# First cross-attention maxima put directly behind the self attention, paired cross units, and four setup products moved to the prologue

## The chip, the core and the metric

The kernel runs on one core of a Trainium2 chip. A core has five engines that run side by side and meet at semaphores: PE (TensorE, matrix products), DVE (VectorE), ACT (ScalarE), POOL (GpSimd) and SP, which here only issues transfers. The metric is device time in microseconds (us) of the whole kernel. Products are written to PSUM, 8 banks of 128 partitions x 512 f32, and read from there by ACT and DVE.

## The reference

Two layers on x of shape (2, 1024, 256) with a context of shape (2, 77, 256):

```python
# layer 0
x = attention(ln32(x), ln32(x), Wq1, Wkv1, Wo1, bo1) + x      # 16 heads of 16, self: 1024 x 1024
x = attention(ln32(x), context, Wq2, Wkv2, Wo2, bo2) + x      # 16 heads of 16, cross: 1024 x 77
x = geglu_ff(ln32(x), Wff1, bff1, Wff2, bff2) + x             # 256 -> 2 x 1024 -> 256
# layer 1
Q = x @ Wq.T + bq; K = ctx @ Wk.T + bk; V = ctx @ Wv.T + bv   # one head of 256
x = rms_norm(softmax(Q K^T / 16) V @ Wfc.T + bfc + x, norm_w)
```

Both softmaxes of layer 0 subtract the row maximum, which the kernel computes beforehand in a first pass of score products.

## The kernel before

The 2048 tokens are 4 blocks of 512 (16 tiles of 128). The 2 x 16 heads are 8 groups of 4 heads, groups 0 to 3 for the first batch, 4 to 7 for the second. The program is written out by hand, one instruction list for each engine, and each list runs in its order; the lists meet at counted semaphores. The stages, with their place in the profiled execution:

- Prologue (0 to 80 us): loads, first layer norm, projections of q, k and v, which go to scratch memory through SP's queue and come back by head. The first 22 tiles of self scores (`first_scores`) lie between them.
- Self attention (80 to 440 us): for each group 16 steps of four transposed score tiles (L915), exponentials (ACT, L1308) and weighing (L927); beside them the score tiles and maxima (L746, DVE L1562) of the next group.
- Cross attention (440 to 563 us). For a group G: four `scores_2` (L1022) with a maximum each (`reduce_2`, DVE L1780); `split_max` (L1568, L1570) turns the result into two halves; `turn_max_2` (L1058) transposes it; `max_copy_2` (ACT L1359) copies it to mT; `load_max_2` (SP L532, two transfers) puts it below the queries in the stack, and only then may `scores_t2` (L1033) of that group start. Its product goes through the exponential (`exp_2`, ACT L1366), `weigh_2` (L1041), a copy (L1372), a transpose (`turn_out_2`, L1052) and `attended_2` (DVE L1718, L1724).
- Feed-forward (563 to 717 us), with each product taken as three of reduced-precision parts, so weights and inputs are split into high and low halves beforehand (`w1_high` on ACT L1342, `w1_low` on DVE L1766, wff2 on POOL L619 and L621). Then layer 1 to 752 us.

Between the attentions and the layer after them stands the chain: a generator `chain(n, b)` for attention n and batch b, from which the engines take pieces at places given by tables. A piece is the transposes of a block (L699; before the products they turn the attention's output, after them the normalised tokens), one product of a tile with Wo (L888, on DVE followed by an addition and the statistics of the norm), or, for n = 0, one projection of the cross queries (`project`, L713; ACT L1223 and DVE L1551 write it, SP L444 stores it, and SP L460 loads it by head, `load_q2`). The DVE's norm steps for a block are short, and are fed one at a time into its list by `tick()`; `finish_norm()` runs what is left of them. The cross stage has units, 8 to a group; PIECES_1 and PIECES_2 say how many pieces follow each unit, AHEAD and FIRST_S2 how many stand ahead of the first. The nine setup products of layer 1 (`final_setup`, L828) are fed in at SETUP_UNITS. Scores of the cross units alternate between two PSUM banks, 4 and 5. A group's q is loaded into one of four slots, so groups 4 to 7 wait until the slot is free.

SP's queue is strictly in order too, so a load waits behind whatever the queue waits for; `parts_stored` holds it until stores have landed.

## Time and profile before

| | us |
|---|---|
| median of 3 runs | 752.19 (751.94 to 753.55) |
| the profiled execution, its own time | 753.79 |
| its span, first to last instruction | 751.8 |
| PE busy | 666.3 (89%) |
| DVE busy | 542.8 (72%) |
| ACT busy | 496.7 (66%) |
| POOL busy | 81.0 (11%) |

The span is 2.0 us below the execution's own time, which is 1.6 us above the median. Busy shares are means over the whole kernel: a stage is read from the table by stretch and the timeline.

### The profile page before, as it was taken

What the parts mean: (1) busy time and instruction counts of PE and PEld (TensorE: products, weight loads), DVE (VectorE), ACT (ScalarE), POOL (GpSimd) and SP (SyncE); (2) the same over time, 40 slices, a digit from 0 to 9 for tenths busy, and PEclk for the clock granted to TensorE, in tenths of its full rate; (3) what the DMA queues carried; (4) which work ended last, traced back from release to release, by engine and by line L of the source; (5) the groups of instructions that cost most, each with busy time, mean ns of one, the idle gap of its engine ahead of it and who ended that gap; (6) DMA issues with size and microseconds to landing.
All of it is one profiled execution on the core that took longest, in us unless ns stands there. A gap on an engine that the chain in (4) does not pass through costs nothing.

```text
span 751.8 us, 11175 instructions
## 1 busy us (share of the span) xinstructions
PE 666.3 (89%) x4072; PEld 319.0 (42%) x4072; DVE 542.8 (72%) x937; ACT 496.7 (66%) x893; POOL 81.0 (11%) x124
## 2 busy tenths in 40 slices
PE   4989799999999999999999873989979999999981
PEld 2644122222222222222224341445537888888870
DVE  6778989999999999999973548465654954343367
ACT  3543299999999999999998730666664333233374
POOL 2080800000000000000000203200020110000004
PEclk9999699999999999999999996899968999999995
DMA  9567440202020100001000021121000000000003
GB/s 295 186 194 230 103 183 1 72 1 71 1 71 2 47 26 1 29 2 29 2 2 1 29 76 38 54 59 34 3 1 1 0 1 1 1 1 1 1 0 112
DMA packets 35114, 36.87 MB, mean 49 GB/s; under 512 B 6133, under 2 KB 28277, under 8 KB 34805
## 3 DMA queue, kind: packets, MB, share of 16 engines
q1 hardware_dynamic: 33904, 35.87, 15.3%
q0 software_dynamic: 1024, 0.24, 0.3%
q8 instruction: 32, 0.52, 0.3%
q14 instruction: 22, 0.17, 0.1%
q10 hardware_dynamic: 132, 0.07, 0.0%
HBM read 23.09 MB, written 12.74 MB: 48 GB/s over the span
## 4 chain that ended last, share of the span: by engine, by line
PE 66%; DVE 15%; ACT 11%; issue 5%; POOL 1%; DMA 0%; ACTq 0%; SPq 0%; DVEq 0%; POOLq 0%
PE ps L927 15%; PE ps L915 10%; DVE mm L1562 7%; ACT probs L1308 6%; PE ps L713 6%; PE ps L1112 4%; PE ps L1113 4%; PE ps L1114 4%; PE ps L746 3%; PE ps L888 3%; PE ps L699 2%; PE ps L1041 2%; PE ps L1128 2%; PE ps L1127 2%; PE ps L1129 2%
## 5 line engine op out<-in xcount | busy, mean ns | idle before, releaser
L1308 ACT ACTIVATE probs<-ps,unfit 128x512 f32<-128x512 f32 x512 | 311.7, 691 | 27.9 <-PE ps L915 23.4
L1562 DVE TENSOR_REDUCE mm<-ps 128x2 f32<-128x1024 f32 x256 | 299.5, 1219 | 14.8 <-PE ps L746 10.8
L915 PE MATMUL ps<-stack 50*128 50x512 f16 x512 | 147.2, 389 | 7.0 <-ACT probs L1308 1.0
L927 PE MATMUL ps<-probs,v 128*32 128x512 f32 x1024 | 138.0, 611 | 2.7 <-ACT outT L1313 2.7
L746 PE MATMUL ps<-stack 48*128 48x512 f16 x512 | 109.1, 392 | 12.7 <-DVE mm L1562 6.6
L915 PEld LDWEIGHTS ps<-stack 50*128 50x128 f16 x512 | 36.9, 93 | 173.0 <-ACT probs L1308 164.1
L1421 ACT ACTIVATE early<-ps,cols 128x512 f32<-128x512 f32 x32 | 22.1, 690 | 90.8 <-PE ps L1114 90.8
L1831 DVE SCALAR_TENSOR_TENSOR hid<-ps,cols,early 128x512 f32<-128x512 f32 x32 | 24.0, 750 | 70.7 <-PE ps L1114 70.5
L1366 ACT ACTIVATE probs<-ps,unfit 96x512 f32<-96x512 f32 x64 | 42.2, 681 | 25.5 <-PE ps L1033 25.2
L1112 PE MATMUL ps<-x_hi,wff_hi 128*128 128x512 f32 x128 | 52.6, 411 | 0.0
L1113 PE MATMUL ps<-x_lo,wff_hi 128*128 128x512 f32 x128 | 51.2, 400 | 0.0
L1114 PE MATMUL ps<-x_hi,wff_lo 128*128 128x512 f32 x128 | 50.9, 398 | 0.0
L746 PEld LDWEIGHTS ps<-stack 48*128 48x128 f16 x512 | 26.2, 94 | 54.3 <-DVE mm L1562 30.5
L612 POOL TENSOR_TENSOR x<-x,rows 128x1024 f32<-128x1024 f32 x12 | 28.2, 2357 | 186.1 <-DVE tok L1540 186.0
L927 PEld LDWEIGHTS ps<-probs,v 128*32 128x32 f32 x1024 | 20.7, 108 | 41.2 <-issue 30.7
L1127 PE MATMUL ps<-wff_hi,hid_hi 128*128 128x256 f32 x128 | 36.4, 285 | 0.0
L1128 PE MATMUL ps<-wff_lo,hid_hi 128*128 128x256 f32 x128 | 36.1, 282 | 0.0
L1657 DVE TENSOR_TENSOR x<-ps,x 128x256 f32<-128x256 f32 x48 | 19.0, 418 | 23.5 <-PE ps L888 21.1
L888 PE MATMUL ps<-wo,wkv 128*128 128x256 f32 x128 | 33.6, 394 | 2.6 <-ACT wkv L1207 1.6
L1129 PE MATMUL ps<-wff_hi,hid_lo 128*128 128x256 f32 x128 | 35.8, 279 | 0.0
L1780 DVE TENSOR_REDUCE mm<-ps 128x8 f32<-128x616 f32 x32 | 25.5, 797 | 12.1 <-PE ps L1022 11.5
L646 POOL TENSOR_SCALAR mu<-mm 128x16 f32<-128x16 f32 x13 | 3.3, 254 | 287.1 <-DVE mm L1578 287.1
(168 smaller groups left out, 875.4 us busy)
## 6 DMA issues: line engine op xcount, KB each, us to landing
v_groups<-early SPq DMA_DIRECT2D x8, 512.0 KB, 3.1
stack<-q_parts SPq DMA_DIRECT2D x64, 64.0 KB, 2.1
v<-v_groups SPq DMA_DIRECT2D x8, 512.0 KB, 4.1
x<-in_x SPq DMA_DIRECT2D x4, 512.0 KB, 8.0
q_parts<-probs SPq DMA_DIRECT2D x8, 256.0 KB, 4.0
k_parts<-probs SPq DMA_DIRECT2D x8, 256.0 KB, 2.2
stack<-k_parts SPq DMA_DIRECT2D x16, 128.0 KB, 2.6
stack<-q_parts SPq DMA_DIRECT2D x64, 32.0 KB, 1.9
```

What stands on the lines that cost most here:

```text
L746: mm_ = eng.matmul(ps[:, 2 * s_slot(G, j, i) + tile, :], qs[rows_i, slot, half, q, P * t:P * t + P], stack[rows_i, SLOTS + slot, q, BLK * ...
L888: mm_ = eng.matmul(ps[:, out_bank(k), 0:D], attT[i // TPB][:, c, P * t:P * t + P], w[:, c, :], start=(c == 0), stop=(c == NC - 1))
L915: eng.matmul(ps[:, st_bank(n), :], stack[rows_of(tile, KROWS), SLOTS + slot, q, P * kc:P * kc + P], qs[rows_of(tile, KROWS), slot, half, q ...
L927: mm_ = eng.matmul(ps[32 * h:32 * h + 32, PV, :], v1[:, G % 2, kc, 32 * h:32 * h + 32], probs[:, k % 2, h, :], start=(kc == 0), stop=(kc = ...
L1112: eng.matmul(ps[:, bank, :], wh, xh[:, c, :], start=(c == 0), stop=False)
L1113: eng.matmul(ps[:, bank, :], wh, xl[:, c, :], start=False, stop=False)
L1114: mm_ = eng.matmul(ps[:, bank, :], wl, xh[:, c, :], start=False, stop=(c == NC - 1))
L1127: eng.matmul(out, hh, w2h, start=(f == 0), stop=False)
L1128: eng.matmul(out, hh, w2l, start=False, stop=False)
L1129: mm_ = eng.matmul(out, hl, w2h, start=False, stop=(f == FC - 1))
L1308: eng.activation(probs[:, k % 2, HEADS[h], :], ps[:, st_bank(n), :], ACT.Exp, scale=unfit[:, 0:1]).then_inc(exp_done, 1)
L1562: eng.tensor_reduce(dst, ps[:, 2 * slot:2 * slot + 2, :], AX.X, ALU.max).then_inc(s_red, 1)
```

## The change

Five things are edited.

1. Behind the self attention the first `scores_2` come after one chain piece (before: after six), and five pieces stand ahead of the first unit (before: ten). Queries of groups 0 and 1 are loaded in two halves, each as soon as its block is stored.
2. A cross unit is now a pair of heads: two products into banks 4 and 5 and one exponential over both (96 partitions x 1024). There are four units to a group, and the products of a unit wait until the exponential of the unit before has read both banks. `scores_2` run six units ahead; the weighing and turning of a group are placed anew, and the maximum of group G + 1 is turned in unit 2 of group G (before: unit 2 of 8).
3. The four k and v products of `final_setup` are moved to the prologue, with their copies on ACT instead of DVE; the other five to the units of group 7.
4. The split of wff1 moves from ACT and DVE to POOL, behind POOL's split of wff2. POOL adds the bias in pieces of two tiles instead of four.
5. The last group's second half and the last piece of the chain for batch 0 are moved behind the first feed-forward product. The feed-forward's own pieces start two products later.

```diff
-        CHAIN_1, CHAIN_2 = 17, 12
-        TAIL = (1, 1, 1, 1, 1, 2, 1, 2, 1, 2, 2, 2)
-        AHEAD, FIRST_S2 = 6, (0, 1, 0, 1, 0, 1, 0, 1) + (0,) * 8
...
-        UNITS = 8
...
-        PIECES_1 = ((1, 0, 1, 0, 1, 0, 1, 0), (1, 0, 1, 0, 1, 0, 0, 0))
-        PIECES_2 = ((0, 0, 0, 0, 0, 0, 0, 1), (1, 0, 1, 0, 1, 0, 1, 0), (1, 0, 1, 0, 1, 0, 1, 0), (1, 0, 1, 0, 1, 0, 0, 0))
-        SETUP_UNITS = ((2, 1), (2, 3), (2, 5), (3, 0), (3, 2), (3, 4), (3, 6), (4, 1), (4, 3))
-        FF_PIECES = (1, 2, 2, 2, 2, 1, 1, 1)
+        CHAIN_1, CHAIN_2 = 16, 12
+        TAIL = (1, 1, 1, 2, 2, 1, 2, 1, 1, 2, 1, 1)
+        UNITS = 4
+        S2_LEAD = 6
+        AHEAD = 5
+        PIECES = ((1, 1, 1, 1), (1, 1, 1, 2), (1, 1, 0, 0), (0, 0, 0, 0),
+                  (0, 0, 1, 1), (1, 1, 1, 2), (1, 1, 1, 1), (0, 0, 0, 0))
+        SETUPS = {(7, 0): 1, (7, 1): 2, (7, 2): 1, (7, 3): 1}
+        SETUP_EARLY = 4
+        FF_PIECES = (0, 0, 2, 2, 2, 2, 2, 2)
...
-            for u in range(PROJ_2, half):
-                store_parts(u)
-            parts_stored(eng, half)
-            for G in range(SLOTS - 1):
-                load_q2(G)
+            for blk in range(2):
+                for u in range(PROJ_2 + NC * blk, PROJ_2 + NC * blk + NC):
+                    store_parts(u)
+                parts_stored(eng, PROJ_2 + NC * blk + NC)
+                for G in range(2):
+                    load_q2(G, (blk,))
+            load_q2(2)
+            load_max_2(0)
             eng.wait_ge(st_full, 64 * GROUPS)
-            load_q2(SLOTS - 1)
-            load_max_2(0)
+            load_q2(3)
             load_max_2(1)
             for u in range(half, half + NC):
                 store_parts(u)
+            load_max_2(2)
             parts_stored(eng, half + NC)
-            for G in range(GROUPS):
...
+            for G in (4, 5):
+                eng.wait_ge(st_full, 64 * GROUPS + UNITS * (G - 3))
+                load_q2(G, (0,))
+            for u in range(half + NC, len(PROJ)):
+                store_parts(u)
+            parts_stored(eng, len(PROJ))
+            load_q2(4, (1,))
+            load_max_2(3)
+            load_q2(5, (1,))
+            eng.wait_ge(st_full, 64 * GROUPS + UNITS * 3)
+            load_q2(6)
+            load_max_2(4)
+            eng.wait_ge(st_full, 64 * GROUPS + UNITS * 4)
+            load_q2(7)
+            for G in range(5, GROUPS):
+                load_max_2(G)
...
-                for blk in range(BLOCKS):
-                    eng.wait_ge(tok_ready, TPB * (BLOCKS * n + blk + 1))
-                    xb = x[:, TPB * blk:TPB * blk + TPB, :]
-                    eng.tensor_tensor(xb, xb, rows[:, row:row + 1, :].to_broadcast([P, TPB, D]), ALU.add).then_inc(bias_added, 1)
+                for i in range(0, TILES, 2):
+                    eng.wait_ge(tok_ready, TILES * n + i + 2)
+                    xb = x[:, i:i + 2, :]
+                    eng.tensor_tensor(xb, xb, rows[:, row:row + 1, :].to_broadcast([P, 2, D]), ALU.add).then_inc(bias_added, 1)
...
+                    parts_stored(eng, len(PROJ))
+                    eng.wait_ge(st_full, 64 * GROUPS)
+                    for f in range(FC):
+                        lo, w, hi = (v[:, :, :, f, :] for v in (wff1_lo, wff1_v, wff1_hi))
+                        eng.tensor_copy(hi, w).then_inc(w1_hi, 1)
+                        eng.wait_ge(w1_hi, f + 1)
+                        eng.tensor_tensor(lo, w, hi.bitcast(F32), ALU.subtract).then_inc(w1_lo, 1)
...
+            eng.wait_ge(w_in["wl1"], 64)
+            for i, w in enumerate((wkT, wvT)):
+                for o in range(NC):
+                    setup(SETUP_1 + NC * i + o, P, B * CTX, [(w[:, c, P * o:P * o + P], ctxT[:, c, :]) for c in range(NC)])
+                    if o == 0:
+                        tile_of_scores()
...
-                tile_of_scores()
+                    eng.wait_ge(su_done, SETUP_1 + SETUP_EARLY)
+                tile_of_scores()
...
+                eng.wait_ge(y_added, TILES + KC)
+                turned(LN3, 0)
+                k = SETUP_1 + SETUP_EARLY
...
+                    if (ln, blk) == (LN3, 1):
+                        eng.wait_ge(su_done, SETUP_1 + SETUP_2)
...
+            def scores_t2(G, d):
+                b, (half, q) = G // GPB, divmod(d, HP)
+                if d == 0:
                     eng.wait_ge(m2_in[G % 4], 16 * HT * (G // 4 + 1))
-                eng.wait_ge(exp_done, 64 * GROUPS + UNITS * G + n - 1)
-                tile, q = divmod(HEADS[h], HP)
-                eng.matmul(ps[0:CTXP, ST + h % 2, :], k2[rows_of(tile, KROWS), b, G % GPB, q, 0:CTXP],
-                           qs[rows_of(tile, KROWS), Q2_SLOT[G % 4], half, q, :], start=True, stop=True).then_inc(st_full, 1)
+                eng.wait_ge(exp_done, 64 * GROUPS + UNITS * G + d)
+                for tile in range(HT):
+                    mm_ = eng.matmul(ps[0:CTXP, ST + tile, :], k2[rows_of(tile, KROWS), b, G % GPB, q, 0:CTXP],
+                                     qs[rows_of(tile, KROWS), Q2_SLOT[G % 4], half, q, :], start=True, stop=True)
+                mm_.then_inc(st_full, 1)
...
-                eng.wait_ge(att_done, EARLY + 2 * GROUPS + max(2 * G - 3, 0))
+                eng.wait_ge(exp_done, 64 * GROUPS - 2)
+                eng.wait_ge(att_done, EARLY + 2 * GROUPS + max(2 * G - 2, 0) - (G == 0))
...
+            def cross_unit(G, d, pieces):
+                scores_t2(G, d)
+                ahead = UNITS * G + d + S2_LEAD
+                if ahead < UNITS * GROUPS:
+                    scores_2(*divmod(ahead, UNITS))
+                advance(pieces, PIECES[G][d] // 2)
+                if d == 0 and G >= 1:
                     weigh_2(G - 1, 1)
-                if n == 2 and G + 1 < GROUPS:
-                    turn_max_2(G + 1)
-                if n == 5 and G >= 1:
+                if d == 1 and G >= 1:
                     turn_out_2(G - 1, 1)
-                if n == 5 and G < GROUPS:
+                if d == 2:
+                    if G + 1 < GROUPS:
+                        turn_max_2(G + 1)
                     weigh_2(G, 0)
-            after_self = chain(0, 1)
-            advance(after_self, AHEAD)
+                if d == 3:
+                    turn_out_2(G, 0)
+                advance(pieces, PIECES[G][d] - PIECES[G][d] // 2)
...
+            after_self, after_cross = chain(0, 1), chain(1, 0)
+            advance(after_self, 1)
+            scores_2(0, 0)
+            scores_2(0, 1)
+            advance(after_self, 2)
+            scores_2(0, 2)
+            scores_2(0, 3)
+            advance(after_self, 1)
+            turn_max_2(0)
+            scores_2(1, 0)
+            scores_2(1, 1)
+            advance(after_self, 1)
...
+                for d in range(UNITS):
+                    cross_unit(G, d, after_self if G < GPB else after_cross)
+                    advance(fillers, SETUPS.get((G, d), 0))
...
-            eng.wait_ge(exp_done, 72 * GROUPS)
+            weigh_2(LAST, 1)
+            last_piece, after_cross = after_cross, chain(1, 1)
+                if n == 0:
+                    turn_out_2(LAST, 1)
+                    advance(last_piece, 1)
...
+            for i, (dst, c0) in enumerate(((kT, COL_BK), (vT, COL_BV))):
+                for o in range(NC):
+                    k = SETUP_1 + NC * i + o
+                    eng.wait_ge(su_full, k + 1)
+                    eng.activation(dst[:, o, :], ps[:, 6 + k % 2, 0:B * CTX], ACT.Identity,
+                                   bias=cols[:, c0 + o:c0 + o + 1]).then_inc(su_done, 1)
...
+            def exp_2(G, d):
+                half, q = divmod(d, HP)
+                eng.wait_ge(st_full, 64 * GROUPS + UNITS * G + d + 1)
+                if q == 0:
                     eng.wait_ge(pv_done, 16 * GROUPS + max(2 * G + half - 1, 0))
-                eng.activation(probs[0:CTXP, half, HEADS[h], :], ps[0:CTXP, ST + h % 2, :], ACT.Exp, scale=unfit[0:CTXP, 1:2]).then_inc(exp_done, 1)
+                eng.activation(probs[0:CTXP, half, q::HP, :], ps[0:CTXP, ST:ST + HT, :], ACT.Exp,
+                               scale=unfit[0:CTXP, 1:2]).then_inc(exp_done, 1)
...
-                        if n == b or blk % 2 == 1:
+                        if n == b:
...
+            def cross_unit(G, d, pieces):
+                ahead = UNITS * G + d + S2_LEAD
+                if ahead < UNITS * GROUPS:
+                    reduce_2(*divmod(ahead, UNITS))
+                advance(pieces, PIECES[G][d] // 2)
+                if d == 1 and G >= 1:
                     attended_2(G - 1, 1)
-            after_self = chain(0, 1)
-            advance(after_self, AHEAD)
-            for n, count in enumerate(FIRST_S2):
-                if n % 2 == 0:
-                    reduce_2(*divmod(n // 2, KC // 2))
-                advance(after_self, count)
-            after_cross = chain(1, 0)
+                if d == 3:
+                    attended_2(G, 0)
+                advance(pieces, PIECES[G][d] - PIECES[G][d] // 2)
```

PE's list behind the self attention, before. L935 is the last transpose of the self attention, L699 turns blocks, L888 is the product with Wo, L1022 the cross scores for the maxima, L1058 the turned maximum, L1033 the first cross unit.

```order
L935 MATMUL ps<-ident,outT 128x128 x4
L699 MATMUL ps<-ident,tok 128x128 x16
L888 MATMUL ps<-wo,wkv 128x256 x8
L1022 MATMUL ps<-k,stack 128x78 x8
L888 MATMUL ps<-wo,wkv 128x256 x2
L1022 MATMUL ps<-k,stack 128x78 x8
L888 MATMUL ps<-wo,wkv 128x256 x2
L1022 MATMUL ps<-k,stack 128x78 x8
L888 MATMUL ps<-wo,wkv 128x256 x2
L1022 MATMUL ps<-k,stack 128x78 x8
L888 MATMUL ps<-wo,wkv 128x256 x2
L1022 MATMUL ps<-k,stack 128x78 x16
```

and now (the same, in this order: L941, L705, L894, L1016, L1054, L1027):

```order
L941 MATMUL ps<-ident,outT 128x128 x4
L705 MATMUL ps<-ident,tok 128x128 x8
L1016 MATMUL ps<-k,stack 128x78 x16
L705 MATMUL ps<-ident,tok 128x128 x8
L894 MATMUL ps<-wo,wkv 128x256 x2
L1016 MATMUL ps<-k,stack 128x78 x16
L894 MATMUL ps<-wo,wkv 128x256 x2
L1054 MATMUL ps<-identh,mpart 96x128
L1016 MATMUL ps<-k,stack 128x78 x16
L894 MATMUL ps<-wo,wkv 128x256 x2
L1027 MATMUL ps<-stack,k 96x512 x2
L1016 MATMUL ps<-k,stack 128x78 x8
```

The sixteen transposes of the two blocks are split by the first two `scores_2`, the maximum of group 0 is turned behind two products instead of eight, and the first unit follows the third product.

SP's queue around the maximum of group 3, before. L444 is a store of cross queries, L532 the load of a maximum, L460 a load of queries.

```order
L444 DMA q_parts<-stack 128x2x512 x2
L532 DMA stack<-mT 2x16x128 x2
L460 DMA stack<-q_parts 32x1024
L460 DMA stack<-q_parts 16x1024
L460 DMA stack<-q_parts 32x1024
L460 DMA stack<-q_parts 16x1024
```

and now (L438, L526 and L454):

```order
L438 DMA q_parts<-stack 128x2x512 x2
L454 DMA stack<-q_parts 32x1024
L454 DMA stack<-q_parts 16x1024
L454 DMA stack<-q_parts 32x1024
L454 DMA stack<-q_parts 16x1024
L526 DMA stack<-mT 2x16x128 x2
```

The load of the maximum, which came directly behind the last stores, now stands behind the wait for their landing and the four loads of group 4's second half.

DVE's list where the norm of the last block before the cross queries ends (L1552 is the low part of a projection, L1541 writes the normalised tokens, L1717 and L1723 are `attended_2`), now:

```order
L1552 SCALAR_TENSOR_TENSOR stack<-ps,fit,stack 128x512
L1717 RECIPROCAL rec<-ps 128x16
L1723 TENSOR_TENSOR tok<-ps,rec 128x4x64
L1515 TENSOR_TENSOR var<-rstd 128x4
L1515 TENSOR_TENSOR var<-var,half_var 128x4
L1518 SCALAR_TENSOR_TENSOR rstd<-var,rstd 128x4
L1515 TENSOR_TENSOR var<-rstd 128x4
L1515 TENSOR_TENSOR var<-var,half_var 128x4
L1518 SCALAR_TENSOR_TENSOR rstd<-var,rstd 128x4
L1541 TENSOR_SCALAR tok<-x,mv,rstd 128x256 x4
```

Before, that block's norm was finished ahead of the first cross unit:

```order
L1514 TENSOR_TENSOR var<-rstd 128x4
L1514 TENSOR_TENSOR var<-var,half_var 128x4
L1517 SCALAR_TENSOR_TENSOR rstd<-var,rstd 128x4
L1540 TENSOR_SCALAR tok<-x,mv,rstd 128x256 x4
L1780 TENSOR_REDUCE mm<-ps 128x2x2x2 x4
L1568 TENSOR_SCALAR mpart<-mm 128x2x16
L1570 SCALAR_TENSOR_TENSOR mpart<-mm,mpart 128x2x16
L1780 TENSOR_REDUCE mm<-ps 128x2x2x2 x2
L1551 SCALAR_TENSOR_TENSOR stack<-ps,fit,stack 128x512
```

The last norm steps have moved behind the low part of the second projection and behind `attended_2`.

## Rows read from the trace of the kernel before

Times are from the span's start.

**Rows 1.** Busy tenths in 40 slices of 18.8 us, from the page:
```profile
PE   4989799999999999999999873989979999999981
PEclk9999699999999999999999996899968999999995
```

**Rows 2.** Table by stretch; columns: us, busy of PE, PEld, DVE, ACT, POOL, clock, DMA:
```profile
440.00:469.60 29.60, 13.70 (x119) 9.61 (x120) 22.24 (x69) 2.34 (x5) 7.10 (x5) 0.81 0.24 64
469.60:483.20 13.60, 13.25 (x86) 6.93 (x86) 5.97 (x10) 9.63 (x17) 5.07 (x5) 0.78 0.12 41
503.70:512.60 8.90, 8.90 (x85) 5.13 (x83) 6.01 (x15) 6.33 (x13) 0.00 (x0) 1.00 0.20 47
533.70:544.00 10.30, 9.43 (x51) 4.62 (x50) 6.44 (x30) 6.44 (x13) 0.00 (x0) 1.00 0.01 2
544.00:562.90 18.90, 13.79 (x63) 6.02 (x62) 11.14 (x35) 11.61 (x20) 4.71 (x2) 0.68 0.00 1
562.90:583.00 20.10, 19.36 (x85) 15.96 (x85) 9.66 (x20) 9.62 (x16) 0.00 (x0) 0.88 0.00 1
```

**Rows 3.** Longest waits, 440 to 563; columns: total, times, longest:
```profile
ACT mT L1359 <- PE ps L1058: 22.4, 1, 22.4
PE ps L1022 <- DVE mm L1780: 13.7, 7, 8.3
```

**Rows 4.** Groups of instructions, 440 to 563, on ACT and DVE:
```profile
L1366 ACT ACTIVATE probs<-ps,unfit 96x512 f32<-96x512 f32 x64 | 42.2, 681 | 25.5 <-PE ps L1033 25.2
L1780 DVE TENSOR_REDUCE mm<-ps 128x8 f32<-128x616 f32 x32 | 25.5, 797 | 12.1 <-PE ps L1022 11.5
```

**Rows 5.** Chain in order of time, cross stage; columns: start, us, what:
```profile
513.13 1.00 PE ps L1041 x8
528.20 1.06 PE ps L888 x4
503.49 0.59 PE ps L1052 x4
497.82 0.72 PE ps L828 x4
```

**Rows 6.** Timeline of PE, cross stage: eight transposes, one projection:
```profile
521.10 1.09 PE L699 MATMUL ps<-ident,tok 128*128 128x128 f32 x8
487.08 1.94 PE L713 MATMUL ps<-xT,wq 128*128 128x512 f32 x4
```

**Rows 7.** Groups of instructions, whole run: copies of two widths on ACT:
```profile
L1351 ACT ACTIVATE x_hi<-xT 128x1024 fp32r<-128x1024 f32 x4 | 4.2, 1050 | 0.0
L1412 ACT ACTIVATE hid_hi<-hid 128x512 fp32r<-128x512 f32 x32 | 19.9, 621 | 1.0 <-DVE hid L1831 1.0
```

**Rows 8.** Timeline of SP's queue and PE, 490 to 494:
```profile
490.97 1.29 SPq L532 DMA_DIRECT2D stack<-mT  x2
492.95 3.56 SPq L460 DMA_DIRECT2D stack<-q_parts  x8
493.57 0.41 PE L1033 MATMUL ps<-stack,k 50*96 50x512 f16 x1 [0.59 <-DMA stack<-mT]
```

**Rows 9.** Table by stretch, PE's pause at 548 and behind it:
```profile
548.00:550.00 2.00, 0.00 (x0) 0.00 (x0) 1.66 (x11) 2.00 (x4) 0.14 (x1) 1.00 0.00 0
552.00:562.00 10.00, 8.22 (x32) 2.90 (x32) 3.39 (x7) 5.79 (x9) 2.21 (x1) 0.50 0.01 2
```

**Rows 10.** Timeline of POOL and DVE at 457, and POOL's weight split:
```profile
456.92 2.34 POOL L612 TENSOR_TENSOR x<-x,rows 128x1024 f32<-128x1024 f32 x1 [31.43 <-DVE tok L1540]
456.96 2.34 DVE L1570 SCALAR_TENSOR_TENSOR mpart<-mm,mpart 128x32 f16<-128x32 f32 x1
L621 POOL TENSOR_TENSOR wff_lo<-wff,wff_hi 128x512 fp32r<-128x512 f32 x4 | 5.1, 1278 | 0.3
```

**Rows 11.** Timeline of DVE in the prologue; PE at the self attention's end:
```profile
78.88 13.66 DVE L1562 TENSOR_REDUCE mm<-ps 128x2 f32<-128x1024 f32 x12
431.85 1.98 PE L713 MATMUL ps<-xT,wq 128*128 128x512 f32 x4 [1.56 <-ACT xT L1212]
```

225 lines of the change are left out of this document (67 added, 158 removed).

## The prediction

> **What bounds the kernel now.** I read the page's slices first, then the table by stretch, the waits, the chain and last the timeline at single places. In the slices [rows 1] PE is at 8 or 9 tenths almost everywhere, with two exceptions: slices 24 and 25 (around 440 to 470 us), where PE is at 7 and 3 and the clock falls to 0.6 and then 0.8, and the slices near 550. The table by stretch [rows 2] gives them sizes. From the last output of the self attention (440.0) to the first cross exponential (469.6) lie 29.6 us with PE busy for 13.70 and DVE for 22.24: neither full. The waits say why [rows 3]: ACT waits 22.4 us once for the turned maximum of group 0, and PE waits 8.3 us in one piece for a maximum of DVE, whose list holds additions and norm steps between the maxima. That is a latency, not a rate, and it is where this change can gain. The eight cross groups then take 93.3 us (469.6 to 562.9). Group 0 takes 13.6 at clock 0.78, group 3 takes 8.9 with PE busy for 8.90 (PE-bound), group 7 takes 18.9 with PE busy for 13.79 at clock 0.68. The first 20.1 us of the feed-forward run at PE 19.36, clock 0.88 [rows 2]: PE-bound, but partly at half clock.
>
> **Part 1, the early first maxima.** From 440.0: eight transposes, 1.1 [rows 6]. The first two `scores_2` need only half 0 of the queries. Each is followed by a maximum of 0.80 [rows 4]; with about 0.6 for its product (a bare group is 6.0 of PE: 8.9 less four setup products of 0.72 [rows 2, 5]; less two weighings of 1.00 and two turns of 0.59 [rows 5] leaves 2.8 for four `scores_2` and eight unit products, so one `scores_2` is under 0.7) and no buffer to spare, two in a row need 1.4 each. So 441.1 + 2.8 = 443.9, the second turn and a product lying beside the maxima. The next two need half 1 of the queries: the last projection of block 1 ends at 433.8 [rows 11]; writing its parts is about 1.5, and store and reload are a transfer each of up to 3.56 [rows 8], which gives 442.4, with other loads in the queue about 445.2 (442.4 to 449). Then 2.8 for two maxima, a product and `split_max` 1.5: the maximum is turned at 449.5. A copy of 0.5 (half of the 1.05 of a wide one [rows 7]) and 2.6 from the load's issue to the first product (490.97 to 493.57 [rows 8]) give 452.6, so the first exponential ends the stretch at about 453 after 13.3 us. **-16.3** (-12 to -19). DVE's 22.24 are no bound against it: most of its work there is moved into groups 0 and 1.
>
> **Part 2, pairs.** An exponential of 512 is 0.681 [rows 4]. ACT's copies cost 1.050 for 1024 and 0.621 for 512 [rows 7]: 0.43 more for the second half, so 1.10 for a pair (bounds 1.05 as the copy, 1.37 as two singles). ACT falls by about 0.25 a pair, but it wasn't the bound. What is new is that the pair uses both banks, so exponential and next product alternate: 1.10 + 0.42 (the product of 0.41 in [rows 8], clock full) = 1.5 a unit. And the maximum of group G + 1 is turned in unit 2, with one unit left behind it: from the products of unit 2 to those of the next group's unit 0 lie 1.10 (the copy stands behind the exponential), 0.5 and 2.6 of transfer, and 0.2 for the turn: 4.4. Two units of 1.5, 4.4, and about 0.6 where weighings and transposes don't fit the gaps: **8.0 for a bare group**, where before it was 6.0 of PE. Pieces come on top, unless they fill gaps. By group:
>
> - G0: four products of 0.53 (1.06 for two [rows 5]) = 2.1, POOL's collision 0.9: 11.0.
> - G1: product, turn, two projections of 1.94 [rows 6], turn = 6.6, of which 1.3 fills gaps: 13.3. The second turn needs the norm of block 3, whose last steps now stand behind the second projection's low part and `attended_2` in DVE's list; PE comes there first and waits about 3.2 (0 to 5): 16.5.
> - G2: two projections 3.9, 1.3 in gaps: 10.6. The maximum of group 3 now stands on SP behind the landing of all stores and four loads. Store and landing about 2.4 (0.4 issue and 2.0 in flight), four loads 1.8, its own transfer 2.6 behind the end of the low part: 6.8 later, and PE has 2.4 of work left: 4.4 of waiting (2 to 6). 15.0.
> - G3: 8.0 + POOL 0.9 = 8.9. G4: a turn and a product, 9.9. G5: five pieces, 11.6. G6: four products, 10.2.
> - G7: no `scores_2`, no second weighing, four units of 1.5, five setup products between 0.72 [rows 5] and 1.94 [rows 6], taken at 1.1: 11.2.
>
> Sum 94.3. The two pauses in G1 and G2 are as long as the one at 548, behind which the clock was 0.50 for the whole of 552 to 562 [rows 9]: 10 us with 8.22 busy, about 4 of them lost; as half of these groups isn't PE-bound I take 3 for both (0 to 8). 97.3 against 93.3: **+4.0** (-6 to +14). What used to make group 0 and group 7 long (clock, wait for the norm of the last block, 18.9) is mostly gone, and the paired loop eats it.
>
> **Part 3, setups.** Four setup products leave the PE-bound middle (4 x 0.72 = 2.9, already in the groups above) and enter the prologue between score tiles, where DVE is the bound: twelve maxima in 13.66 us [rows 11], 1.14 each, one after the other. They hide behind those, except where they use the banks of a score tile; their copies move to ACT, idle there. +0.8 (0 to 2). At the end of the self attention the wait of 1.56 for `xT` [rows 11] goes, since another piece stands there: -1.5 (0 to -1.6). **-0.7.**
>
> **Part 4, POOL.** Taking wff1's split from ACT and DVE gives nothing by itself: neither bounds the stretches where it stood (DVE 11.14 and ACT 11.61 of 18.9 in group 7 [rows 2]). POOL has time: four subtractions of 1.28 [rows 10] for wff2 and eight more, with copies, end at about 500, 45 us before the first use. But POOL and DVE collide: POOL's addition of 2.34 and DVE's L1570 of 2.34 start together and end together [rows 10], although L1570 has 32 elements per partition, and I take its normal length as below 0.25. Each such meeting costs DVE up to 1.3 beside a subtraction of 1.28, and only the one that meets `split_max` is in the max loop: 0.9 in two groups, as above (0 to 1.3 a group in all eight at worst). The Trainium skill (GPSIMD Engine Reference, section 1, Specifications) says that POOL's SBUF interfaces are shared with VectorE, with contention for DVE instructions in a fast mode or with two SBUF inputs; L1570 has two SBUF inputs, and the trace agrees with its 2.34. By that rule the one-input half of `split_max` is spared and the price is paid once per group; by the row alone it could be either.
>
> **Part 5, the feed-forward.** The clock is at full when it starts, as PE has no pause near its end: 0.88 over 20.1 us means 24% of it, 4.8 us, at half clock [rows 2], half of that is lost: -2.4. Copies of `attended_2` and of the weight split ahead of its first products go: -0.7. A turn of 0.59 [rows 5] and a turn of eight transposes 1.09 [rows 6] now stand behind the first product: +1.7. **-1.4** (-3 to +2).
>
> **The sum** is made against the profiled execution, 753.79, whose span is 751.8 and which is 1.6 above the median of 752.19: -16.3 + 4.0 - 0.7 - 1.4 = -14.4, so 739.4 for such an execution and 737.8 for a median: **738**. First feed-forward product then at about 440 - 0.7 + 13.3 + 97.3 = 550.
>
> **Rivals.**
> (a) The loop doesn't bind. If the maximum's transfer is hidden by pieces and both pauses stay under 2 us, the clock stays at full, groups cost their PE work, 4 to 9 us less in all: 728 to 733. For it: bare groups before ran at PE 8.90 of 8.90. Against it: before had six units of eight behind the turn, now one of four.
> (b) The loop costs more. With pairs at 1.37, the pauses at their upper bounds and the clock down twice, +4 to +10: 742 to 749. For it: the clock fell behind both long pauses of before [rows 1, 9].
> (c) The other side: slower. Every group has the pause in front of its unit 0, and the clock never comes back in the cross stage. The place is L1027's wait for the maximum's load; the price is a group at half clock, 13.6 at a mean of 0.78 in [rows 2], about 14.5 at 0.5, so 8 x 14.5 = 116 against 93.3, +22.7, less 16.3 and 1.4 to 2: +4 to +6, 756 to 758. It decides from 1.8 us of additional time in each of eight groups on top of mine (14.4 / 8). For it: a loop of 4.4 with 1.5 of PE work in it in bare groups; against it: PE works in between (weighing, `scores_2`, pieces), and the pauses in bare groups are about 2 in pieces, shorter than those behind which the clock fell. The Trainium skill (TensorE: Matmul & The Clock Gate, HAM oscillation) speaks for this: it describes kernels whose PE waits for loads again and again and that swing between the clocks; of before, the trace shows it only behind the two long pauses.
> (d) No change: what is gained at the front only makes the stage wait elsewhere, for instance for the queries of groups 1 and 2, which come from projections that stand in G1 and G2 now; each group would lose 1.8 more. Nothing in the rows shows such a wait, since q of group 2 is loaded whole before its turn: 751 to 753.
>
> **Chances.** Forecast, 732 to 744: 0.55. (a) 0.13, (b) 0.14, (c) 0.12, (d) 0.06. A change of 0.2%, 1.5 us, is about what a measurement of this kernel can tell from none. (a), the forecast and (b) are faster, 0.82; (d) is 0.06; (c) 0.12. The range goes over (a) and (b), 727 to 751, and leaves out (c), some of (d) and the tails of the rest.
>
> **What the profile of the changed kernel would show.** Part 1: the first 96 x 1024 exponential at 450 to 456; near 469 it is wrong. Pairs: a mean of 1.05 to 1.15. Loop: waits of PE (L1027) for the load of stack<-mT in groups 3 to 7, below 2 each, and one of 4 to 5 ahead of group 3; if that one is missing, the order on SP costs nothing. G1: PE (L705) waits for DVE's L1541 by about 3. Clock below 1 in two or three slices between 470 and 510; if it is low from 460 to 550, it is (c). POOL: L1571 stretched beside POOL's subtractions. First feed-forward product at 545 to 555, the clock at 1 there, and the feed-forward itself 154 less 1 to 3. I am wrong above all if the groups sum to under 88 or over 106.

## The result, and the profile after

| | before | after |
|---|---|---|
| median | 753.39 (7 runs) | 760.17 (7 runs, 756.52 to 762.28) |
| the profiled execution, its own time | 753.79 | 756.86 |
| its span | 751.8 | 754.8 |

The changed kernel is slower by 1.0%: ratio 1.0097, interval 1.0077 to 1.0117. The prediction said 738. The prediction's range ended at 751. The two profiled executions differ by only 3.0, since the one of after is among the faster of its seven; the stretches below add up to these 3.0, and the rest of the 6.8 between the medians stands in no profile. The slices of PE and of its clock after, to be held against [rows 1]:

```profile
PE   4999899999999999999999878769979999999981
PEclk9999799999999999999999977775999999999995
```

The hole of slices 24 and 25 (7 and 3 before, 7 and 8 after) is gone, but slices 26 and 27 are at 7 and 6 instead of 9 and 8, and slices 24 to 28 have a clock of 7, 7, 7, 7 and 5, where before it was 9, 6, 8, 9 and 9. The table by stretch, with the columns of [rows 2]: the start of the cross stage, groups 0 to 7, and the feed-forward with all behind it.

```profile
438.20:453.90 15.70, 10.98 (x88) 7.11 (x87) 7.70 (x16) 2.49 (x6) 0.00 (x0) 0.68 0.29 84
453.90:464.80 10.90, 10.90 (x74) 5.94 (x69) 7.57 (x29) 5.16 (x6) 0.00 (x0) 0.68 0.07 17
464.80:485.70 20.90, 14.10 (x101) 7.21 (x97) 14.39 (x42) 9.93 (x14) 5.84 (x6) 0.90 0.13 42
485.70:503.80 18.10, 12.30 (x78) 4.53 (x73) 6.07 (x12) 6.77 (x10) 11.34 (x13) 0.78 0.16 51
503.80:514.70 10.90, 9.59 (x73) 3.94 (x67) 5.82 (x10) 5.85 (x7) 10.08 (x11) 0.50 0.19 57
514.70:527.20 12.50, 12.33 (x93) 6.56 (x91) 4.97 (x12) 7.94 (x12) 0.00 (x0) 0.56 0.08 25
527.20:537.20 10.00, 9.88 (x85) 5.76 (x77) 7.50 (x21) 5.68 (x8) 0.00 (x0) 1.00 0.01 3
537.20:548.20 11.00, 9.72 (x77) 4.95 (x71) 10.48 (x41) 7.22 (x9) 2.54 (x2) 1.00 0.01 2
548.20:557.80 9.60, 9.50 (x59) 4.57 (x54) 4.39 (x13) 6.40 (x8) 0.00 (x0) 1.00 0.01 2
557.80:754.80 197.00, 171.42 (x992) 149.00 (x988) 98.22 (x236) 75.83 (x168) 17.21 (x18) 0.94 0.03 11
```

and the last of these before:

```profile
562.90:751.80 188.90, 167.69 (x978) 146.59 (x977) 99.16 (x232) 76.69 (x171) 13.11 (x14) 0.94 0.04 12
```

| stretch | before | after | change | predicted |
|---|---|---|---|---|
| start to last self output | 440.0 | 438.2 | -1.8 | -0.7 |
| to the first cross exponential | 29.6 | 15.7 | -13.9 | -16.3 |
| eight cross groups | 93.3 | 103.9 | +10.6 | +4.0 |
| first feed-forward product to end | 188.9 | 197.0 | +8.1 | -1.4 |

So the 14 us at the front are there. They are spent again in groups 1 and 2 (20.9 and 18.1), in groups 3 and 4, which run at or near half clock (0.50 and 0.56), and in the feed-forward. Three pauses of PE stand at these places (timeline of PE; in brackets the idle time before the row and what ended it):

```profile
481.82 1.03 PE L705 MATMUL ps<-ident,tok 128*128 128x128 f32 x3 [3.34 <-DVE tok L1541]
503.12 0.66 PE L1027 MATMUL ps<-stack,k 50*96 50x512 f16 x2 [5.65 <-DMA stack<-mT]
564.44 0.89 PE L705 MATMUL ps<-ident,tok 128*128 128x128 f32 x3 [3.13 <-DVE tok L1541]
```

DVE's timeline tells how the third comes about. Its list waits for the last `turn_out_2`, which this change puts behind the first feed-forward product, and the last steps of a norm stand behind that wait, though nothing they need is missing:

```profile
556.93 0.42 DVE L1746 COPY vw<-ps 77x256 f32<-77x256 f32 x1
561.34 0.26 DVE L1717 RECIPROCAL rec<-ps 128x16 f32<-128x16 f32 x1 [3.99 <-PE ps L1047]
561.98 0.15 DVE L1518 SCALAR_TENSOR_TENSOR rstd<-var,rstd 128x4 f32<-128x4 f32 x1
...
563.88 2.33 DVE L1541 TENSOR_SCALAR tok<-x,mv,rstd 128x256 f32<-128x256 f32 x4
```

The pause at 481 is of the same kind: DVE idles for 2.99 until ACT has copied a projection, while the norm's steps stand behind that wait.

```profile
473.26 0.15 DVE L1515 TENSOR_TENSOR var<-var,half_var 128x4 f32<-128x4 f32 x1
476.40 0.75 DVE L1552 SCALAR_TENSOR_TENSOR stack<-ps,fit,stack 128x512 f16<-128x512 f32 x1 [2.99 <-ACT stack L1233]
```

### The profile page after: what moved, and what is told of

The parts are those of the page before. It is cut to its first block, busy times and chain, and to the rows that moved or that the text cites. A ratio compares the mean times of both kernels' runs of the same rounds, so it can differ in the third digit from the quotient of the medians.

```text
span 754.8 us, 11161 instructions
## 1 busy us (share of the span) xinstructions
PE 670.4 (89%) x4072; PEld 321.9 (43%) x4072; DVE 536.9 (71%) x925; ACT 491.0 (65%) x857; POOL 99.2 (13%) x152
## 3 DMA queue, kind: packets, MB, share of 16 engines
q0 software_dynamic: 1024, 0.24, 0.3%
## 4 chain that ended last, share of the span: by engine, by line
PE 65%; DVE 17%; ACT 11%; issue 5%; DMA 1%; POOL 1%; SPq 0%; ACTq 0%; DVEq 0%; POOLq 0%
PE ps L933 15%; PE ps L921 10%; DVE mm L1563 7%; PE ps L719 6%; ACT probs L1322 6%; PE ps L1119 4%; PE ps L1120 4%; PE ps L1121 4%; PE ps L894 4%; PE ps L752 4%; PE ps L705 2%; PE ps L1036 2%; PE ps L727 2%; PE ps L1135 2%; PE ps L1134 2%
## 5 line engine op out<-in xcount | busy, mean ns | idle before, releaser
L1563 DVE TENSOR_REDUCE mm<-ps 128x2 f32<-128x1024 f32 x256 | 299.4, 1219 | 13.9 <-PE ps L752 10.0
L612 POOL TENSOR_TENSOR x<-x,rows 128x512 f32<-128x512 f32 x24 | 31.7, 1333 | 167.5 <-DVE tok L1541 167.4
L1377 ACT ACTIVATE probs<-ps,unfit 96x1024 f32<-96x1024 f32 x32 | 35.5, 1109 | 26.8 <-PE ps L1027 26.7
L894 PE MATMUL ps<-wo,wkv 128*128 128x256 f32 x128 | 37.9, 433 | 1.8 <-DVE x L1658 1.1
L705 PE MATMUL ps<-ident,tok 128*128 128x128 f32 x160 | 26.1, 304 | 14.3 <-DVE tok L1541 9.7
```

The costliest lines, as they stand in the source:

```text
L894: mm_ = eng.matmul(ps[:, out_bank(k), 0:D], attT[i // TPB][:, c, P * t:P * t + P], w[:, c, :], start=(c == 0), stop=(c == NC - 1))
L1563: eng.tensor_reduce(dst, ps[:, 2 * slot:2 * slot + 2, :], AX.X, ALU.max).then_inc(s_red, 1)
```

## The experiments

Each ran beside the kernel before on its chip; the ratio is to that, with its 95% interval. The changed kernel's own is 1.0097. All are edits of the changed kernel. "G" is a cross group.

**e1: the load of maximum 3 ahead on SP.**

```diff
-            parts_stored(eng, len(PROJ))
-            load_q2(4, (1,))
             load_max_2(3)
+            parts_stored(eng, len(PROJ))
+            load_q2(4, (1,))
```

> The changed kernel with one load moved: on SP the load of group 3's maximum stands ahead of the wait for the stores' landing and of group 4's loads. Theory 'pauses' (the loss is three PE pauses that the new order makes, and the half clock behind each): PE's wait of 5.65 us at 497.5 to 503.1 shrinks to under 2 us and the half clock of 500 to 522 goes with it, so 5 for the wait and 5 to 7 for the clock: 8 to 12 us below the changed kernel, about 750 against its 760. Rival 'pairs' (the loss is the alternation of exponential and product over both banks, with one unit behind the turned maximum): the wait shrinks, but group 3 and 4 stay near 11 and 12 us, and the time falls by at most 3.

757.08, ratio 1.0047 (1.0021 to 1.0074): some 4 us won, not 8 to 12. The wait shrank as expected, and another took its place. From PE's timeline:

```profile
500.92 0.66 PE L1027 MATMUL ps<-stack,k 50*96 50x512 f16 x2 [1.36 <-DMA stack<-mT]
504.37 0.44 PE L1016 MATMUL ps<-k,stack 48*128 48x78 f16 x8 [2.78 <-DMA stack<-q_parts]
```

The queries for `scores_2` (4, 2) come from projections that this change puts into units 0 and 1 of G2, with only two units between them and their use in unit 0 of G3. Group 3 stayed at half clock (13.5 us).

**e3: both norms finished at once, as before; e4: e1 and e3 together; e5: e4, and the last half ahead of the feed-forward.**

```diff
-                        if n == b:
+                        if n == b or blk % 2 == 1:
                             finish_norm()
```

> The changed kernel with the norms of the second and fourth block finished at once again, as in the kernel before, instead of one step at a time between other work of DVE. Theory 'pauses': PE's waits for L1541 go (3.3 + 0.8 at 481, 3.1 + 0.9 at 563, 1.1 + 0.6 at 606: 9 to 10 us in all) and with them the half clock of 482 to 492, 561 to 570 and around 606 (about 4 + 2 + 2): 10 to 16 us below the changed kernel; some 2 us may come back where the norm's 4.3 us of DVE now delay a maximum. Rival 'pairs': at most 4 us, since the groups are bound by their own loop.

> Both edits together: the load of group 3's maximum ahead of the stores' landing, and the two norms finished at once. Theory 'pauses': the effects add, 18 to 25 us below the changed kernel, about 738 to 742, that is faster than the kernel before by 1.5 to 2%; clock 1.0 from 464 to the feed-forward. Rival 'pairs': 5 us at most, still not faster than the kernel before.

> As the kernel with both edits, and the last group's second half and the last chain piece stand ahead of the first feed-forward product again. If that move alone made the pause of 561 to 564, this kernel is the one that loses it and is 2 to 4 us below the kernel with both edits; if the late norm made it (theory 'pauses' as I read it), the two are within 1.5 us of each other, and this one may be slower by up to 2, since PE then waits for the copy and the division of the last half with nothing in between.

762.03, 759.75 and 764.85; ratios 1.0100 (1.0039 to 1.0161), 1.0107 (1.0055 to 1.0158) and 1.0154 (1.0098 to 1.0210), from four runs each. My theory missed: none is faster than the changed kernel. The stretch from the first feed-forward product is short again in e3, 189.0 against 197.0, so the late norm did make the pause that ends at 564. But G1 takes 25.7 and G7 14.0. The waits of PE in e3, 450 to 575, say why:

```profile
PE ps L1016 <- DVE mm L1761: 9.1, 5, 4.9
PE ps L1027 <- DMA stack<-mT: 7.5, 2, 5.8
PE ps L1047 <- issue: 2.9, 1, 2.9
```

The wait for the norm has become one of 4.9 for a maximum, which stands behind the norm's chain in DVE's list. These steps take 4.7 us of DVE here (474.95 to 479.67) and 3.8 in the kernel before (460.79 to 464.55), so the place must be one where neither a maximum nor a turn is waited for. In e5 group 7 grows further, to 16.1, as the last half's turn then stands in it with nothing between it and its copy.

**e6: the norms in DVE's idle times.**

```diff
                     if n == 0:
+                        if b == 1:
+                            finish_norm()
                         for o in range(NC):
                             remainder(u)
...
+            finish_norm()
             attended_2(LAST, 1)
```

> The changed kernel with DVE's list altered in two places: the norm of the last block is finished directly ahead of the first low part of its batch's projections (where DVE idles 3 us behind the maxima), and the norm in front of the last `attended_2` is finished ahead of DVE's wait for it. PE's order is as in the changed kernel. Theory 'norm latency' (new, after the kernel that finished the norms at once only moved PE's wait from the turn to a maximum): the norm of a block is 4.3 us of DVE that must stand where nobody waits; here both pauses go (3.3 + 0.8 at 481, 3.1 + 0.9 at 563) and the half clock behind them, so group 1 takes 16 to 17.5 instead of 20.9 and the stretch from the first feed-forward product to the end 189 to 191 instead of 197; SP's pause of 5.7 ahead of group 3 stays. 8 to 13 us below the changed kernel. Rival 'pairs': under 4.

751.08, ratio 0.9972 (0.9953 to 0.9992), 9 us below the changed kernel. G1 is 18.7 (16 to 17.5 was expected), and both waits for L1541, at 481 and 564, are gone. The feed-forward and all behind it:

```profile
558.10:748.70 190.60, 169.68 (x992) 148.25 (x988) 98.00 (x234) 75.83 (x168) 17.25 (x18) 0.94 0.04 12
```

**e7: e6, and the last block's projections in G1 instead of G2** (SP stores and loads them ahead of group 5's queries).

```diff
-        PIECES = ((1, 1, 1, 1), (1, 1, 1, 2), (1, 1, 0, 0), (0, 0, 0, 0),
+        PIECES = ((1, 2, 1, 1), (1, 1, 2, 2), (0, 0, 0, 0), (0, 0, 0, 0),
```

> As the kernel before it in this list, and the two projections of the last block stand in group 1 instead of group 2, with their stores and loads on SP ahead of the loads for group 5 and of the maximum of group 3. The kernel with that maximum moved alone showed that behind its wait stood another, of 2.8, for the queries of group 4's second half. Theory 'latency chain': projection, store, landing and load need some 9 us before `scores_2` (4, 2) in unit (3, 0); with the projections three units earlier both waits at 497 to 504 are under 1 each and the clock stays at 1.0 from about 465 on. Groups: 11, 20 (two projections more), 9, 8.5, 10, 10, 11, 9.6, about 89 in all against 104; time 18 to 24 us below the changed kernel, 736 to 742, and faster than the kernel before. Rival 'pairs': groups 2 to 4 stay at 11 and more each and the time stays above 752.

747.53, ratio 0.9927 (0.9903 to 0.9951): 12.6 below the changed kernel, not 18 to 24. The wait for the queries is gone, the one for maximum 3 is still 5.6, because I had left it behind eight loads for group 5, and those behind the four for group 4. SP's timeline, where L526 is that maximum:

```profile
493.49 6.29 SPq L454 DMA_DIRECT2D stack<-q_parts  x12
499.82 1.27 SPq L526 DMA_DIRECT2D stack<-mT  x2
```

**e8: e7 with the pairs undone. e9: e7 with wff1's split back on ACT and DVE.**

```diff
                 for tile in range(HT):
+                    eng.wait_ge(st_full, 64 * GROUPS + 2 * (UNITS * G + d) + tile + 1)
...
+                    eng.activation(probs[0:CTXP, half, q + HP * tile, :], ps[0:CTXP, ST + tile, :], ACT.Exp,
```

> As the kernel with both edits, with the pairs undone: each of a unit's two products has its own exponential of 512 and waits for its own bank alone. This prices the pairing by itself. ACT has 32 x (1.36 - 1.11) = 8 us more to do, PE waits less for the banks. Theory 'latency chain': pairs aren't the loss, so the time is within 3 us of the kernel with pairs, on either side. Rival 'pairs': 5 to 15 us faster than the kernel with pairs.

> As the kernel with both edits, with the split of wff1 given back to ACT and DVE (group 7 and the first feed-forward products). Theory 'latency chain': POOL's split isn't the loss; DVE's maxima beside POOL cost under 1.3 each in groups 3 and 4, and ACT and DVE pay about 1 to 2 in group 7: within 2 us of the kernel with both edits. Rival 'port': DVE is slowed by POOL's 16 instructions so much that this one is 3 us or more faster.

747.78, ratio 0.9931 (0.9913 to 0.9949), and 748.25, ratio 0.9922 (0.9892 to 0.9952): both are e7 within their intervals. So neither the pairs nor POOL's split is a loss that these intervals (some 2 us to either side) can show.

**e10: e7, and maximum 3 ahead of group 5's queries, whose own wait for group 1 goes with it. e12: e10 with ten pieces ahead of the first unit instead of five.** This takes the early first unit back, but not the early maxima: the first `scores_2` still stand behind one piece, not six.

```diff
-            eng.wait_ge(st_full, 64 * GROUPS + UNITS * 2)
-            load_q2(5)
             load_max_2(3)
+            load_q2(5)
...
-        AHEAD = 5
+        AHEAD = 10
...
+        PIECES = ((1, 1, 1, 1), (1, 1, 0, 0), (0, 0, 0, 0), (0, 0, 0, 0),
```

> As the kernel with the norms in DVE's holes and the projections in group 1, and on SP the load of group 3's maximum stands ahead of the eight loads for group 5 (in that kernel these eight, 0.45 us each on the queue, made PE wait 5.6 us at 496.8). Theory 'latency chain': that wait shrinks to under 1.5, the clock stays at 1.0 behind it, so groups 3 and 4 take about 8.5 and 10 instead of 10.1 and 11.7: 5 to 9 us below that kernel's 747.5, about 740. Rival 'pairs': the wait comes back in front of groups 4 and 5, and the time falls by 2 at most.

> As the first kernel of this list, but five more chain pieces (the other five products with their additions and norm) stand ahead of the first cross unit, ten as in the kernel before; so the first exponential comes some 10 us later and group 0 and 1 have five pieces fewer. This undoes the headline of the change and leaves the rest. Theory 'the work is only moved' (new): the 22 us of DVE ahead of the first unit in the kernel before were the additions, statistics and norms of the chain; started early, the units wait for them in groups 0 and 1. Then this kernel is within 4 us of the first. Rival 'the early start is worth its length': this kernel is 8 to 12 us slower.

743.73, ratio 0.9875 (0.9854 to 0.9895), and 745.27, ratio 0.9886 (0.9847 to 0.9926). G2 falls from 12.9 to 8.8 in e10, but groups 3 and 4 stay at 10.5 and 11.5 with a clock of 0.50 and 0.62, so it is 3.8 below e7 and not 5 to 9. In e12 the first exponential comes at 465.8, 7.8 later, and the first feed-forward product 6.7 later in the two profiled executions, but the medians are 1.5 apart and the intervals overlap. (In the profiled execution of e12 the self attention had already ended 3 later.) So the early first unit by itself is worth at most some 5 us, and by the medians 1.5. Most of what it shows at the front is work moved from one side of the first exponential to the other. No run puts the maxima back behind six pieces, so what they are worth alone is not shown.

**e11 and e13: the changed kernel with useless products in its first two pauses** (one of them is 0.88 us; nothing reads their result). e11 has 7 and 11 of them, e13 has 4 and 6.

```diff
+            def keep_busy(G, d, count):
+                eng.wait_ge(exp_done, 64 * GROUPS + UNITS * G + d)
+                for _ in range(count):
+                    eng.matmul(ps[:, ST, :], wql[:, 0, 0:P], wkv2[:, 0, 0:512], start=True, stop=True)
```

> The changed kernel itself with 18 products added that nothing reads: 7 on PE ahead of the last block's turn in unit (1, 3) and 11 ahead of the first product of group 3, 0.48 us each, so that PE is busy for 3.4 and 5.3 us in the two pauses in which it waited for the norm and for the maximum's load. They prolong nothing if they fit. Theory 'pauses cost twice' (waiting, and the half clock behind it): the waits stay, the clock is at 1.0 from about 465 to 560, group 2 takes 14 to 15 instead of 18, groups 3 and 4 about 9 and 10 instead of 10.9 and 12.5: 5 to 8 us below the changed kernel, about 752 to 755. Rival 'waiting alone': the clock changes, but the groups are bound by exponentials, transfers and maxima, so at most 2 us.

> The changed kernel with useless products in its two long pauses again, fitted to them: one such product took 0.88 us and not 0.48, so the 7 and 11 of the kernel before ran 2.8 and 3.7 us past the pauses. Now 4 (3.5 us) ahead of the last block's turn and 6 (5.3 us) ahead of group 3. The pauses themselves stay. Theory 'pauses cost twice': groups 1 to 4 take 20.9, 15.5, 9 and 11, that is 6 us less than in the changed kernel, whose median is 757 to 760: about 752. Rival 'waiting alone': within 2 us of the changed kernel.

e11: 757.12, ratio 1.0062 (1.0041 to 1.0083): 3 us below the changed kernel and not 5 to 8, as its products ran 6.5 us past the pauses. e13: 754.34, ratio 1.0015 (0.9991 to 1.0039), 0.8% or 6 us below the changed kernel, as expected. Through the first pause and group 2 the clock holds; groups 3 and 4 still lose it:

```profile
480.00:500.00 20.00, 17.21 (x109) 7.95 (x109) 13.06 (x28) 10.53 (x14) 10.08 (x10) 1.00 0.22 74
505.60:515.20 9.60, 7.64 (x71) 3.32 (x65) 5.74 (x10) 5.77 (x8) 9.20 (x11) 0.74 0.19 54
515.20:526.90 11.70, 11.54 (x92) 5.87 (x91) 5.05 (x12) 7.94 (x12) 0.10 (x1) 0.63 0.11 27
```

PE has more to do and the kernel is faster: what is won here is the clock alone, since the transfer and the norm that PE waited for come no earlier by it. The Trainium skill (TensorE: Matmul & The Clock Gate, HAM oscillation) describes this, a load that PE waits for in mid-kernel and half clock behind it. Here the trace of the changed kernel agrees: 0.50 through group 3, behind the wait of 5.65.

**e14: e10 with a useless product at the head of eight units, (2, 2) to (4, 1). e15: e10 with the five late setup products back in groups 2 and 3.** The waits that hold these five, and those behind them, are placed anew with them.

```diff
+                    if tile == 0 and (2, 2) <= (G, d) <= (4, 1):
+                        eng.matmul(ps[:, ST, 0:D], wql[:, 0, 0:P], wkv2[:, 0, 0:D], start=True, stop=True)
...
-        SETUPS = {(7, 0): 1, (7, 1): 2, (7, 2): 1, (7, 3): 1}
+        SETUPS = {(2, 1): 1, (2, 3): 1, (3, 0): 1, (3, 2): 1, (3, 3): 1}
```

> The best kernel so far (norms in DVE's holes, projections in group 1, maximum 3 first; 743.7 us) with one useless product of about 0.45 us at the head of each unit from (2, 2) to (4, 1), eight in all. In that kernel no pause is longer than 2.3 us, and yet the granted clock is 0.5 from 493 to 516, where PE was busy for about 83% before it fell. Theory 'bare groups don't hold the clock' (without setup products, group 2 to 4 have too little work on PE): the added work of 3.6 us raises it, the clock is 1.0 there, groups 3 and 4 take 9 and 10 instead of 10.5 and 11.5, and the time falls by 1 to 3 although PE has more to do. Rival 'no': PE's 3.6 us are simply added, 746 to 747.

> The same best kernel with the five late setup products moved from group 7 back to groups 2 and 3, where the kernel before had them. Theory 'bare groups don't hold the clock': as in the kernel with useless products the clock stays at 1.0, groups 2 to 4 take 9.5, 10 and 10; in group 7 (9.6 now) the norm ahead of the feed-forward is then uncovered, which costs 2 to 3 of the 5 that the products took there: 3 to 5 us below 743.7. Rival 'group 7 needs its cover': group 7 stays at 9 and more, with a pause behind which the feed-forward starts at half clock, and the time is the same or above.

e14: median 739.25, ratio 0.9861 (0.9815 to 0.9908), but in two kinds: four executions of 738.7 to 739.3 at a mean clock of 0.967, two of 748.4 at 0.949 (the profiled one is of the second kind). The first kind is 4.5 us below e10, the second 4.7 above it. So the fill seems to help in the executions whose clock is higher, and doesn't hold the clock always; there is no profile of the first kind, and over all six executions the interval overlaps that of e10. e15: 737.77, ratio 0.9799 (0.9775 to 0.9823), the fastest kernel here, 2.0% below the kernel before. Its group 3, group 4 and group 7:

```profile
496.50:510.10 13.60, 12.33 (x85) 5.89 (x83) 6.03 (x13) 5.91 (x7) 10.45 (x12) 0.75 0.31 80
510.10:518.70 8.60, 7.69 (x95) 4.53 (x93) 4.89 (x11) 7.33 (x11) 0.00 (x0) 1.00 0.03 7
539.70:547.20 7.50, 5.11 (x39) 1.52 (x31) 3.49 (x13) 6.39 (x8) 0.00 (x0) 1.00 0.00 0
```

Against e10, group 7 fell by 2.2 to 7.4, with the clock at 1.00, so it didn't need its cover. Group 3 is 3.1 longer, 13.6 instead of 10.5 (it has three of the setup products and a clock of 0.75), and group 4 is 2.9 shorter, 8.6 instead of 11.5, at a clock of 1.00. Group 2, with the other two, takes 8.1 instead of 8.8. So groups 2 to 4 take in the five products, some 5.5 us of PE at full clock, in 30.3 us instead of 30.8. The two profiled executions are 3.1 apart, the medians 6.0.

## Why the prediction was wrong

**Part 1 was right, as a stretch.** From the last self output to the first exponential it is 15.7 instead of the forecast 13.3: PE waits five times there, for maxima, a copy and a division, 0.7 to 1.3 each, and the clock is 0.68. That the first exponential starts at 453.86 (453 was forecast) is in part luck: in e1, e11 and e13, whose programs are the same up to there, it starts at 456.8, 456.8 and 459.5, since the self attention ends later. What failed is the sentence on DVE: "DVE's 22.24 are no bound against it: most of its work there is moved into groups 0 and 1". It was moved, but I priced it at one wait of 3.2. DVE's busy time from the last self output to the end of G1 shows that it is mostly the same work: 22.24 + 5.97 [rows 2] + 5.56 = 33.8 before, 7.70 + 7.57 + 14.39 = 29.7 after. G1 before was:

```profile
483.20:494.40 11.20, 9.30 (x72) 3.66 (x71) 5.56 (x12) 7.30 (x15) 0.00 (x0) 1.00 0.22 73
```

By the end of G1 the kernel before had done all sixteen pieces and the changed kernel fourteen. From the last self output to there it was 54.4 us before and 47.5 after; the two projections that were left took 3.78 and 1.88 in G2. That leaves 1.2 us of the 14, and e12 shows the same from the other side.

**Part 2, the groups, failed in the size of G1 to G4:** forecast 16.5, 15.0, 8.9 and 9.9, and 3 for the clock, measured 20.9, 18.1, 10.9 and 12.5. In G1 the pause for the norm was forecast at 3.2 and measured at 3.34 + 0.80, and PE also waits 1.58 and 0.33 for maxima and 0.75 for a division there, for the same reason as in part 1: DVE's list is full. In G2 the SP wait was forecast at 4.4 and measured at 5.65, and the first projection took 3.78 at half clock instead of 1.94; that makes up the 3.1. Groups 3 and 4 ran at a clock of 0.50 and 0.56. I had allowed 3 us for the clock; e13 prices the part behind the two pauses at 6.

G0 came out at 10.9 (11.0), but by luck. The sum took a product with Wo as 0.53, half of the 1.06 of [rows 5]. That row is one product already: it has 4 records, and each of the eight products ahead of G2 is such a row of 4 in the timeline after. So G0 has 4.2 us of products at full clock and not 2.1, PE is busy for all of its 10.9, and the loop of 8.0 and POOL's 0.9 didn't come on top of them. The same error stands in G1, G4, G5 and G6. In G5 to G7, at a clock of 1.00, the two errors cancel too: 10.0, 11.0 and 9.6 measured, 11.6, 10.2 and 11.2 forecast. The pair's exponential is as forecast, 1.10 (32 of them, 1109 ns):

```profile
L1377 ACT ACTIVATE probs<-ps,unfit 96x1024 f32<-96x1024 f32 x32 | 35.5, 1109 | 26.8 <-PE ps L1027 26.7
```

That exponential and product alternate over both banks costs nothing that e8 can show. The bare group was sized nearly right: group 2 of e10, which has no long wait, took 8.8 at a clock of 0.73, with 8.0 forecast.

**Part 3** can't be resolved. The first self step starts at 81.9 after and at 84.0 before, but at 83.6 and 84.3 in e6 and e10, whose prologue is the changed kernel's. The miss was to count 2.9 us as saved where the moved setup products had stood, in groups 2 and 3. e15 shows for the five late ones that groups 2 to 4 take them in for nothing, and the median falls by 6 us when they stand there and not in group 7. For the four that went to the prologue no run shows it.

**Part 4** was right that the split of wff1 gives nothing in sum (e9). On collisions it looked at the wrong instruction. L1571 has a median of 193 ns and at most 528 after, where the kernel before had one of 2342, beside an addition of POOL twice as wide.

```profile
L1571 DVE SCALAR_TENSOR_TENSOR mpart<-mm,mpart x11: 174/193/528, 76.8 to 542.0; 128x32 f16<-128x32 f32 x8, 128x16 f16<-128x16 f32 x3
L1570 DVE SCALAR_TENSOR_TENSOR mpart<-mm,mpart x11: 174/192/2342, 78.8 to 532.8; 128x32 f16<-128x32 f32 x8, 128x16 f16<-128x16 f32 x3
```

But POOL's addition of two tiles now starts while DVE still normalises the block's other two, and one of these four instructions takes 1.38 instead of 0.41. From the timelines of DVE and POOL after, and of DVE before:

```profile
481.27 2.33 DVE L1541 TENSOR_SCALAR tok<-x,mv,rstd 128x256 f32<-128x256 f32 x4
482.08 1.36 POOL L612 TENSOR_TENSOR x<-x,rows 128x512 f32<-128x512 f32 x1 [12.51 <-DVE tok L1541]
550.39 1.38 DVE L1540 TENSOR_SCALAR tok<-x,mv,rstd 128x256 f32<-128x256 f32 x4
```

PE's second waits of 0.80 and 0.94 for L1541 come from that. The 24 instructions of this line between 440 and 620 take 13.7 us after and 8.5 before, and I had no term for it. In every run POOL adds the bias in pieces of two tiles, so what they cost in sum is not shown. Nor are one-input instructions spared, as the prediction thought possible for the half of `split_max`: L1569, that half, takes 0.99 once in the cross stage (507.63, beside POOL's subtraction of 1.27) and 0.18 in the other seven.

**Part 5 is the step with the wrong sign,** -1.4 forecast, +8.1 measured. The clock at the start of the feed-forward is 1.0 as forecast, and the 1.7 of moved turns is there. But I costed the move on PE alone and didn't follow it into DVE's list, where the norm of a block stands behind the wait for the moved turn. It makes PE wait for 3.13 + 0.94 at 561 to 566 and start at half clock again. e6 moves those norm steps and gets 6.4 of the 8.1 back. The 2.4 that I credited to the clock and the 0.7 for copies are not seen even then: e6 has a clock of 1.00 over the first 19.9 us of the feed-forward, and the stretch takes 190.6 against 188.9 before.

The rival for the other side, (c), had the right sign and part of the mechanism: half clock in groups 3 and 4, but from two long pauses and not from one in every group, and groups 5 to 7 run at 1.00. The chance given to it was 0.12. What stays open is how much of the clock's fall in groups 3 and 4 is due to the thin work there and how much to timing that differs from run to run; e14's two kinds show that it isn't fixed by the program alone.

## What to carry to other kernels

Before work is moved past a wait on one engine, write down what the other engines' lists have behind their part of that wait; a chain of small steps (here a norm of some 4 us) belongs in a hole of its engine, and neither ahead of a maximum nor behind something its engine waits for. Work that is moved out of an idle stretch is not saved unless it lands beside something. Before a row of a profile is divided by a count, check what one unit of the program leaves in it. Price a pause of PE twice, with what runs at half clock behind it, and keep small independent products for thin stretches.
